# Selective scan: every fourth state's drive multiplied by POOL from a copy in SBUF

## The chip, the cores and the metric

The kernel runs on one core of a Trainium2 chip. The metric is the device time of one execution in microseconds; the median of several runs is compared. The engines are PE (TensorE), ACT (ScalarE), DVE (VectorE), POOL (GpSimd) and SP, which here only starts DMAs. They run their own instruction streams and meet at semaphores.

## What is computed

A hybrid layer: a gated selective scan, a feed-forward part with experts, a retention and attention part, and the feed-forward part again, each added to x. The change lies in the selective scan alone:

```python
def step(h, inp):
    dt_t, B_t, C_t, u_t = inp
    dA = jnp.exp(dt_t[..., None] * A)
    h = dA * h + (dt_t * u_t)[..., None] * B_t[:, None, :]
    y = jnp.einsum('bdn,bn->bd', h, C_t)
    return (h, y)
...
v = _silu(x_norm @ v1_w + v1_b)
return x_ssm * v @ w2_w + w2_b
```

There are 4 batches, 1024 time steps, 128 channels d and 16 states n. The second summand, (dt u) B, is called the drive below.

## The kernel before

The channels lie on the 128 partitions and time along the free dimension, so one batch's row is a tile of 128x1024 in f32. `selective_scan` handles one state of one batch after another, 64 in all. For each state n of a batch:

- PE spreads row n of B over the partitions into `drive_ps[n % 2]` (`spread_b`, L552; two PSUM tiles of 128x1024) and row n of C into `c_ps` (`spread_c`, L557). The selecting matrices and the rows are bf16.
- ACT makes `decay` = exp(dt a_n) in SBUF (L615) and copies `c_ps` into `c_rep` in SBUF (L619).
- DVE multiplies `drive_ps[n % 2]` by `du_t` = dt u in place, in PSUM (`drive`, L635), and then runs the scan over time (`scan`, L642) from `decay` (SBUF) and `drive_ps` (PSUM) into `state` (SBUF).
- POOL, which has access to SBUF alone here, multiplies `state` by `c_rep` into `hc` (L685).
- PE adds `hc` into `y_ps` by a product with the identity (`add_state`, three states later).

The order of each engine's work is written out by hand. DVE goes in pairs (`body`, L645): two scans, then the drives of the next two states. `spread_b` of state n waits until the scan of state n-2 has read the tile (L554), `spread_c` waits for ACT's copy of the state before. Count objects turn a batch and a state into the value that a semaphore must have. `pipelined` (L470) lets the last states of a batch overlap with the first ones of the next; at such a change of batch DVE also makes `y_sb` (L661), `yv` (L655) and the addition to x (L665), and PE the product with w2.

Beside it the expert weights are split into a high and a low f16 part, two experts a batch, at the states named in `SPLITS` = (3, 11): ACT's `enlarge` (L602) after its copy of c for state 3, ACT's `high_part` (L607) after that of state 4, POOL's `low_part` (L677) after `hc` of state 5, and the same from state 11. SP stores the result.

Semaphore waits stand in the stream of the waiting engine: what is behind a waiting instruction waits too.

Of the kernel before, what the change touches and what calls it, by code (L numbers as in the profile page):

```python
# [19 lines left out]
ALU = mybir.AluOpType  # L20
ACT = mybir.ActivationFunctionType
# [6 lines left out]
P = 128  # L28
B, T = 4, 1024
# [4 lines left out]
NS = 16  # L34
# [452 lines left out]
def selective_scan(t):  # L487
# [9 lines left out]
    with Stage(nc, "scan") as s:  # L497
        a_neg = s.sb("a_neg", [P, NS])
        dt_b = s.sb("dt_b", [P, T])
        decay = s.sb("decay", [P, 4, T])  # L500
        state = s.sb("state", [P, 2, T])
        c_rep = s.sb("c_rep", [P, 4, T])
        hc = s.sb("hc", [P, 4, T])
        y_sb = s.sb("y_sb", [P, T])
        yv = s.sb("yv", [P, T])
        w_raw, w_large = (s.sb(n, [P, 2, F]) for n in ("w_raw", "w_large"))
# [12 lines left out]
        dt_staged = s.count("dt_staged")  # L519
        decayed = s.count("decayed", NS, 1)  # L520
        c_copied = s.count("c_copied", NS, 1)
        driven = s.count("driven", NS)
        scanned = s.count("scanned", NS, 4)
        weighed = s.count("weighed", NS, 4)
        y_steps = s.count("y_steps", 2, 2)
        projected = s.count("projected", 1, 1)
        added = s.count("added", 1, 1)
        SPLITS = (3, 11)

        with nc.Block() as block:  # L530

# [57 lines left out]
            def _(act):  # L589
# [19 lines left out]
                with act.Fori(0, B) as b:  # L609
                    act.wait_ge(decayed.sem, decayed.before(b, 0, 1))  # L610
                    act.activation(dt_b[:, :], t.dt_t[:, b, :], ACT.Copy).then_inc(dt_staged.sem, 1)
                    act.wait_ge(dt_staged.sem, dt_staged.at(b))
                    for n in range(NS):
                        act.wait_ge(scanned.sem, scanned.before(b, n, 4))
                        act.activation(decay[:, n % 4, :], dt_b[:, :], ACT.Exp,  # L615
                                       scale=a_neg[:, n:n + 1]).then_inc(decayed.sem, 1)
                        act.wait_ge(c_spread.sem, c_spread.at(b, n))
                        act.wait_ge(weighed.sem, weighed.before(b, n, 4))
                        act.activation(c_rep[:, n % 4, :], c_ps[:, :], ACT.Copy).then_inc(c_copied.sem, 1)  # L619
                        if n in SPLITS:  # L620
                            enlarge(b, SPLITS.index(n))
                        if n - 1 in SPLITS:
                            high_part(b, SPLITS.index(n - 1), w_parts)
# [4 lines left out]
            def _(dve):  # L628
# [2 lines left out]
                dve.sem_inc(added.sem, added.start)  # L631

                def drive(b, n):
                    dve.wait_ge(b_spread.sem, b_spread.at(b, n))
                    dve.tensor_tensor(drive_ps[n % 2][:, :], drive_ps[n % 2][:, :], t.du_t[:, b + n // NS, :],  # L635
                                      ALU.mult).then_inc(driven.sem, 1)

                def scan(b, k):
                    dve.wait_ge(driven.sem, driven.at(b, k))
                    dve.wait_ge(decayed.sem, decayed.at(b, k))  # L640
                    dve.wait_ge(weighed.sem, weighed.before(b, k, 2))
                    dve.tensor_tensor_scan(state[:, k % 2, :], decay[:, k % 4, :], drive_ps[k % 2][:, :], 0.0,  # L642
                                           ALU.mult, ALU.add).then_inc(scanned.sem, 1)

                def body(b, n):  # L645
# [25 lines left out]
            def _(pool):  # L671
# [7 lines left out]

                with pool.Fori(0, B) as b:  # L680
                    for n in range(NS):
                        pool.wait_ge(scanned.sem, scanned.at(b, n))
                        pool.wait_ge(c_copied.sem, c_copied.at(b, n))
                        pool.wait_ge(summed.sem, summed.before(b, n, 4))
                        pool.tensor_tensor(hc[:, n % 4, :], state[:, n % 2, :], c_rep[:, n % 4, :],  # L685
                                           ALU.mult).then_inc(weighed.sem, 1)
                        if n - 2 in SPLITS:
                            low_part(b, SPLITS.index(n - 2), w_parts)
# [1266 lines left out]
```

## Time and profile before

| | us |
|---|---|
| median of 3 runs | 1385.3 (1382.85 to 1386.9) |
| the profiled execution | 1391.36 |
| its span | 1389.4 |
| scan stage in it, from the first drive to the last addition to x | 98.6 to 348.0 |
| DVE busy, 97.5 to 345.9 | 227.9 of 248.4 |
| POOL busy, the same stretch | 170.6 |
| ACT busy, the same stretch | 154.2 |
| PE busy, the same stretch | 195.0 |

The rows come from the page of the profile (groups of instructions, with the idle time of the engine just before them and what released it) and from answers of the trace (timelines: start, duration, engine, line, operation, output and inputs). Times are us from the span's start, means are ns. In a timeline an instruction marked x2 is two of them merged, with their common duration; two neighbours on one engine may overlap by some hundredths of a microsecond, so starts are subtracted rather than durations added.

### The profile page before, as it was taken

What the parts mean: (1) busy time and instruction counts of PE and PEld (TensorE: products, weight loads), DVE (VectorE), ACT (ScalarE), POOL (GpSimd) and SP (SyncE); (2) the same over time, 40 slices, a digit from 0 to 9 for tenths busy, and PEclk for the clock granted to TensorE, in tenths of its full rate; (3) what the DMA queues carried; (4) which work ended last, traced back from release to release, by engine and by line L of the source; (5) the groups of instructions that cost most, each with busy time, mean ns of one, the idle gap of its engine ahead of it and who ended that gap; (6) DMA issues with size and microseconds to landing.
All of it is one profiled execution on the core that took longest, in us unless ns stands there. A gap on an engine that the chain in (4) does not pass through costs nothing. (4 is left out here: it accounts for less than half of the span.)

```text
span 1389.4 us, 17492 instructions
## 1 busy us (share of the span) xinstructions
PE 1071.3 (77%) x5850; PEld 393.9 (28%) x5850; DVE 742.7 (53%) x1012; ACT 975.3 (70%) x884; POOL 325.7 (23%) x194
## 2 busy tenths in 40 slices
PE   4748777777799956777446888888888888679996
PEld 3213333333344422332341111111111111134443
DVE  5869998987566648998481001200300300256664
ACT  3767665754688832221336999999999999658885
POOL 3117776766111114665100000000000000011110
PEclk8769999999899978998777999999999999879998
DMA  2000100100100000000001111111111111000002
GB/s 73 0 16 30 31 30 30 60 30 31 32 30 30 31 24 0 0 0 1 8 0 33 24 24 32 37 24 28 22 33 34 24 24 28 11 31 31 30 30 61
DMA packets 24188, 36.48 MB, mean 26 GB/s; under 512 B 7362, under 2 KB 11970, under 8 KB 24130
## 3 DMA queue, kind: packets, MB, share of 16 engines
q1 hardware_dynamic: 24130, 35.71, 9.5%
q8 instruction: 36, 0.59, 0.2%
q14 instruction: 22, 0.18, 0.0%
HBM read 16.82 MB, written 6.29 MB: 17 GB/s over the span
## 5 line engine op out<-in xcount | busy, mean ns | idle before, releaser
L1674 ACT ACTIVATE att_prob<-att_s_ps 128x1536 f32<-128x1536 f32 x342 | 459.2, 1912 | 7.4 <-PE att_s_ps L1588 7.3
L1603 PE MATMUL att_o_ps<-att_prob,att_va 128*32 128x512 f32 x2048 | 273.9, 607 | 0.5 <-ACT att_prob L1674 0.5
L1705 DVE COPY att_o_sb<-att_o_ps 128x512 f32<-128x512 f32 x32 | 22.1, 691 | 381.7 <-PE att_o_ps L1603 381.7
L1588 PE MATMUL att_s_ps<-att_q_st,att_k_st 32*128 32x512 f16 x1024 | 134.4, 388 | 80.8 <-ACT att_prob L1674 76.1
L685 POOL TENSOR_TENSOR scan_hc<-scan_state,scan_c_rep 128x1024 f32<-128x1024 f32 x64 | 151.9, 2392 | 71.9 <-DVE scan_state L642 71.7
L787 POOL TENSOR_TENSOR ffn_veps<-ffn_mv,all_eps 128x4 f32<-128x4 f32 x16 | 9.1, 570 | 575.3 <-DVE ffn_mv L944 575.3
L642 DVE TENSOR_TENSOR_SCAN scan_state<-scan_decay,scan_drive_ps 128x1024 f32<-128x1024 f32 x64 | 142.9, 2270 | 0.3 <-ACT scan_decay L615 0.3
L282 PE MATMUL scan_y_ps<-scan_hc,all_ident 128*128 128x512 f32 x256 | 130.2, 634 | 8.3 <-DVE scan_y_sb L661 6.2
L1588 PEld LDWEIGHTS att_s_ps<-att_q_st,att_k_st 32*128 32x128 f16 x1024 | 33.1, 91 | 327.2 <-ACT att_prob L1674 315.9
L619 ACT ACTIVATE scan_c_rep<-scan_c_ps 128x1024 f32<-128x1024 f32 x64 | 65.4, 1022 | 80.4 <-PE scan_c_ps L282 80.1
L1012 DVE SCALAR_TENSOR_TENSOR ffn_hid_lo<-ffn_hid,ffn_share,ffn_hid_hi 128x1024 f16<-128x1024 f32 x64 | 81.9, 1283 | 48.8 <-ACT ffn_hid_hi L920 48.1
L1318 POOL TENSOR_TENSOR ret_qm<-ret_mem,ret_q_sb 128x1024 f32<-128x1024 f32 x32 | 74.5, 2350 | 67.0 <-DVE ret_mem L1270 64.0
L916 ACT ACTIVATE ffn_hid<-ffn_h_ps,ffn_be 128x1024 f32<-128x1024 f32 x64 | 71.1, 1111 | 21.7 <-PE ffn_h_ps L292 19.1
L635 DVE TENSOR_TENSOR scan_drive_ps<-scan_drive_ps,ssm_du_t 128x1024 f32<-128x1024 f32 x64 | 77.8, 1220 | 14.7 <-PE scan_drive_ps L282 14.4
L282 PE MATMUL scan_drive_ps<-ssm_bc,ssm_sel 96*128 (+1 forms) x128 | 41.4, 407 | 47.5 <-DVE scan_state L642 37.6
L292 PE MATMUL ffn_o_ps<-ffn_hid_hi,ffn_w_sel 128*128 128x512 f16 x256 | 76.0, 379 | 2.2 <-DVE ffn_hid_lo L1012 2.2
L920 ACT ACTIVATE ffn_hid_hi<-ffn_hid,ffn_share 128x1024 f16<-128x1024 f32 x64 | 73.5, 1149 | 4.9
L292 PE MATMUL ffn_h_ps<-ffn_z_hi,ffn_w_sel 128*128 (+1 forms) x256 | 76.2, 379 | 0.0
L615 ACT ACTIVATE scan_decay<-scan_dt_b,scan_a_neg 128x1024 f32<-128x1024 f32 x64 | 72.9, 1140 | 0.1
L1270 DVE TENSOR_TENSOR_SCAN ret_mem<-ret_g_sb,ret_kv_ps 128x1024 f32<-128x1024 f32 x32 | 71.2, 2266 | 0.0
L282 PEld LDWEIGHTS scan_y_ps<-scan_hc,all_ident 128*128 128x128 f32 x256 | 51.3, 202 | 55.5 <-issue 35.3
L1012 DVE SCALAR_TENSOR_TENSOR ffn_hid_lo<-ffn_hid,all_blend,ffn_hid_hi 128x1024 f16<-128x1024 f32 x32 | 42.9, 1341 | 44.4 <-ACT ffn_hid_hi L920 44.4
(215 smaller groups left out, 1505.8 us busy)
## 6 DMA issues: line engine op xcount, KB each, us to landing
ffn_w_sel<-w_split SPq DMA_DIRECT2D x16, 512.0 KB, 3.2
w_split<-scan_w_parts SPq DMA_DIRECT2D x8, 512.0 KB, 2.9
att_q_st<-hv_part SPq DMA_DIRECT2D x64, 64.0 KB, 2.1
att_k_st<-hv_part SPq DMA_DIRECT2D x64, 64.0 KB, 2.1
ln_x_half<-in_x SPq DMA_DIRECT2D x8, 256.0 KB, 2.8
scan_w_raw<-in_w1e SPq DMA_DIRECT2D x8, 256.0 KB, 3.2
scan_w_raw<-in_w2e SPq DMA_DIRECT2D x8, 256.0 KB, 3.4
out<-store_out SPq DMA_DIRECT2D x8, 256.0 KB, 2.4
```

The source lines that it names most:

```text
L282: last = pe.matmul(out[:, h], w, rhs[:, h], start=start, stop=stop)
L292: last = pe.matmul(out[:, h], w, x[:, h], start=start and i == 0, stop=stop and i == len(parts) - 1)
L615: act.activation(decay[:, n % 4, :], dt_b[:, :], ACT.Exp, scale=a_neg[:, n:n + 1]).then_inc(decayed.sem, 1)
L635: dve.tensor_tensor(drive_ps[n % 2][:, :], drive_ps[n % 2][:, :], t.du_t[:, b + n // NS, :], ALU.mult).then_inc(driven.sem, 1)
L642: dve.tensor_tensor_scan(state[:, k % 2, :], decay[:, k % 4, :], drive_ps[k % 2][:, :], 0.0, ALU.mult, ALU.add).then_inc(scanned.sem, 1)
L685: pool.tensor_tensor(hc[:, n % 4, :], state[:, n % 2, :], c_rep[:, n % 4, :], ALU.mult).then_inc(weighed.sem, 1)
L920: act.activation(hid_hi[:, m % 3, :], hid[:, m % 2, :], ACT.Copy, scale=weight_of_expert(k)).then_inc(casted.sem, 1)
L1012: dve.scalar_tensor_tensor(hid_lo[:, m % 3, :], hid[:, m % 2, :], weight_of_expert(m % M // FC), hid_hi[:, m % 3, :], ALU.mult, ALU.subtra ...
L1318: pool.tensor_tensor(qm[:, n, :], mem[:, n % 2, :], q_sb[:, :], ALU.mult).then_inc(weighed.sem, 1)
L1588: last = pe.matmul(s_ps[e % 2][:, n, :], k_st[rows, g % 2, kc * P:(kc + 1) * P], q_st[rows, g % 2, HALVES[half]], start=True, stop=True)
L1603: last = pe.matmul(o_ps[half][32 * j:32 * j + 32, :], va[:, g % 2, kc, j, :], prob[:, (GH * v + j) % RING, :], start=kc == 0, stop=kc == K ...
L1674: act.activation(prob[:, first % RING:first % RING + n, :], s_ps[e % 2][:, 0:n, :], ACT.Exp).then_inc(exped.sem, 1)
```

## The change

For the states 3, 7, 11 and 15 of each batch the drive no longer is DVE's. ACT copies the spread row from `drive_ps[1]` into a new SBUF tile `b_rep`, POOL multiplies it by `du_t` in place, and DVE's scan of that state reads `b_rep` instead of PSUM. The wait of `spread_b` on the scan two states before is as it was. There is one `b_rep`, so the four uses of a batch follow each other. `SPLITS` becomes (2, 10): enlarging after state 2, high part after 3, low part after 4.

```diff
+        b_rep = s.sb("b_rep", [P, T])
...
-        driven = s.count("driven", NS)
+        driven = s.count("driven", NS - NS // 4)
+        seen = s.sem("seen")
+        b_copied, pool_driven = s.count("b_copied", NS // 4), s.count("pool_driven", NS // 4)
...
-        SPLITS = (3, 11)
+        SPLITS = (2, 10)
+
+        def by_pool(n):
+            return n % 4 == 3
...
                         act.wait_ge(c_spread.sem, c_spread.at(b, n))
                         act.wait_ge(weighed.sem, weighed.before(b, n, 4))
+                        if by_pool(n):
+                            act.wait_ge(b_spread.sem, b_spread.at(b, n))
+                            act.activation(b_rep[:, :], drive_ps[n % 2][:, :], ACT.Copy).then_inc(b_copied.sem, 1)
                         act.activation(c_rep[:, n % 4, :], c_ps[:, :], ACT.Copy).then_inc(c_copied.sem, 1)
...
                 def drive(b, n):
+                    if by_pool(n):
+                        return
...
                 def scan(b, k):
-                    dve.wait_ge(driven.sem, driven.at(b, k))
+                    if by_pool(k):
+                        dve.wait_ge(pool_driven.sem, pool_driven.at(b, k // 4))
+                    else:
+                        dve.wait_ge(driven.sem, driven.at(b, k - k // 4))
                     dve.wait_ge(decayed.sem, decayed.at(b, k))
                     dve.wait_ge(weighed.sem, weighed.before(b, k, 2))
-                    dve.tensor_tensor_scan(state[:, k % 2, :], decay[:, k % 4, :], drive_ps[k % 2][:, :], 0.0,
+                    source = b_rep if by_pool(k) else drive_ps[k % 2]
+                    dve.tensor_tensor_scan(state[:, k % 2, :], decay[:, k % 4, :], source[:, :], 0.0,
...
                     for n in range(NS):
+                        if by_pool(n + 1):
+                            pool.wait_ge(b_copied.sem, b_copied.at(b, n // 4))
+                            pool.sem_inc(seen, 1)
+                            pool.tensor_tensor(b_rep[:, :], b_rep[:, :], t.du_t[:, b, :],
+                                               ALU.mult).then_inc(pool_driven.sem, 1)
                         pool.wait_ge(scanned.sem, scanned.at(b, n))
```

On DVE, in the middle of a batch, four states stand so before (names that end in 0 and 1 are the two PSUM tiles; an instruction named SCALAR_TENSOR_TENSOR with `scan_state` as output is the scan):

```order
L635 TENSOR_TENSOR scan_drive_ps0<-scan_drive_ps0,ssm_du_t 128x1024
L635 TENSOR_TENSOR scan_drive_ps1<-scan_drive_ps1,ssm_du_t 128x1024
L642 SCALAR_TENSOR_TENSOR scan_state<-scan_decay,scan_drive_ps0 128x1024
L642 SCALAR_TENSOR_TENSOR scan_state<-scan_decay,scan_drive_ps1 128x1024
L635 TENSOR_TENSOR scan_drive_ps0<-scan_drive_ps0,ssm_du_t 128x1024
L635 TENSOR_TENSOR scan_drive_ps1<-scan_drive_ps1,ssm_du_t 128x1024
L642 SCALAR_TENSOR_TENSOR scan_state<-scan_decay,scan_drive_ps0 128x1024
L642 SCALAR_TENSOR_TENSOR scan_state<-scan_decay,scan_drive_ps1 128x1024
```

and so with the change:

```order
L646 TENSOR_TENSOR scan_drive_ps0<-scan_drive_ps0,ssm_du_t 128x1024
L646 TENSOR_TENSOR scan_drive_ps1<-scan_drive_ps1,ssm_du_t 128x1024
L657 SCALAR_TENSOR_TENSOR scan_state<-scan_decay,scan_drive_ps0 128x1024
L657 SCALAR_TENSOR_TENSOR scan_state<-scan_decay,scan_drive_ps1 128x1024
L646 TENSOR_TENSOR scan_drive_ps0<-scan_drive_ps0,ssm_du_t 128x1024
L657 SCALAR_TENSOR_TENSOR scan_state<-scan_decay,scan_drive_ps0 128x1024
L657 SCALAR_TENSOR_TENSOR scan_state<-scan_decay,scan_b_rep 128x1024
```

The second drive of every other pair is gone, and the scan that it fed reads `b_rep`.

On POOL, states 10 to 15 of a batch stand so before:

```order
L685 TENSOR_TENSOR scan_hc<-scan_state,scan_c_rep 128x1024
L685 TENSOR_TENSOR scan_hc<-scan_state,scan_c_rep 128x1024
L685 TENSOR_TENSOR scan_hc<-scan_state,scan_c_rep 128x1024
L685 TENSOR_TENSOR scan_hc<-scan_state,scan_c_rep 128x1024
L677 TENSOR_TENSOR scan_w_parts<-scan_w_large,scan_w_parts 128x2x512
L685 TENSOR_TENSOR scan_hc<-scan_state,scan_c_rep 128x1024
L685 TENSOR_TENSOR scan_hc<-scan_state,scan_c_rep 128x1024
```

and so with the change:

```order
L700 TENSOR_TENSOR scan_b_rep<-scan_b_rep,ssm_du_t 128x1024
L705 TENSOR_TENSOR scan_hc<-scan_state,scan_c_rep 128x1024
L705 TENSOR_TENSOR scan_hc<-scan_state,scan_c_rep 128x1024
L705 TENSOR_TENSOR scan_hc<-scan_state,scan_c_rep 128x1024
L692 TENSOR_TENSOR scan_w_parts<-scan_w_large,scan_w_parts 128x2x512
L705 TENSOR_TENSOR scan_hc<-scan_state,scan_c_rep 128x1024
L700 TENSOR_TENSOR scan_b_rep<-scan_b_rep,ssm_du_t 128x1024
L705 TENSOR_TENSOR scan_hc<-scan_state,scan_c_rep 128x1024
L705 TENSOR_TENSOR scan_hc<-scan_state,scan_c_rep 128x1024
```

The product for state 11 stands ahead of `hc` of state 10, that for state 15 ahead of `hc` of state 14, and `low_part` moved from behind state 13 to behind state 12.

## Rows read from the trace of the kernel before

**Rows 1.** The page's groups: xcount | busy us, mean ns | idle before, releaser.
```profile
L685 POOL TENSOR_TENSOR scan_hc<-scan_state,scan_c_rep 128x1024 f32<-128x1024 f32 x64 | 151.9, 2392 | 71.9 <-DVE scan_state L642 71.7
...
L642 DVE TENSOR_TENSOR_SCAN scan_state<-scan_decay,scan_drive_ps 128x1024 f32<-128x1024 f32 x64 | 142.9, 2270 | 0.3 <-ACT scan_decay L615 0.3
...
L619 ACT ACTIVATE scan_c_rep<-scan_c_ps 128x1024 f32<-128x1024 f32 x64 | 65.4, 1022 | 80.4 <-PE scan_c_ps L282 80.1
...
L635 DVE TENSOR_TENSOR scan_drive_ps<-scan_drive_ps,ssm_du_t 128x1024 f32<-128x1024 f32 x64 | 77.8, 1220 | 14.7 <-PE scan_drive_ps L282 14.4
```

**Rows 2.** Timeline, 129 to 143 us: start, us, engine, instruction [idle before].
```profile
129.03 4.46 DVE L642 TENSOR_TENSOR_SCAN scan_state<-scan_decay,scan_drive_ps 128x1024 f32<-128x1024 f32 x2
...
133.40 2.42 DVE L635 TENSOR_TENSOR scan_drive_ps<-scan_drive_ps,ssm_du_t 128x1024 f32<-128x1024 f32 x2
...
133.95 0.60 PE L282 MATMUL scan_drive_ps<-ssm_bc,ssm_sel 96*128 x2
...
135.01 1.02 ACT L619 ACTIVATE scan_c_rep<-scan_c_ps 128x1024 f32<-128x1024 f32 x1 [0.52 <-PE scan_c_ps L282]
...
135.72 4.46 DVE L642 TENSOR_TENSOR_SCAN scan_state<-scan_decay,scan_drive_ps 128x1024 f32<-128x1024 f32 x2
...
138.08 4.69 POOL L685 TENSOR_TENSOR scan_hc<-scan_state,scan_c_rep 128x1024 f32<-128x1024 f32 x2 [2.02 <-DVE scan_state L642]
...
140.05 1.05 ACT L607 ACTIVATE scan_w_parts<-scan_w_large 128x1024 f16<-128x1024 f32 x1
...
142.04 1.01 ACT L619 ACTIVATE scan_c_rep<-scan_c_ps 128x1024 f32<-128x1024 f32 x1
...
142.43 4.45 DVE L642 TENSOR_TENSOR_SCAN scan_state<-scan_decay,scan_drive_ps 128x1024 f32<-128x1024 f32 x2
```

**Rows 3.** Timeline at two changes of batch, DVE and PE.
```profile
173.43 4.45 DVE L642 TENSOR_TENSOR_SCAN scan_state<-scan_decay,scan_drive_ps 128x1024 f32<-128x1024 f32 x2
...
177.52 2.68 PE L282 MATMUL scan_y_ps<-scan_hc,all_ident 128*128 128x512 f32 x4
...
231.90 1.23 DVE L635 TENSOR_TENSOR scan_drive_ps<-scan_drive_ps,ssm_du_t 128x1024 f32<-128x1024 f32 x1 [1.87 <-PE scan_drive_ps L282]
...
234.24 4.46 DVE L642 TENSOR_TENSOR_SCAN scan_state<-scan_decay,scan_drive_ps 128x1024 f32<-128x1024 f32 x2
```

**Rows 4.** Timeline of POOL, `low_part` behind a pair of `hc`.
```profile
149.42 2.13 POOL L677 TENSOR_TENSOR scan_w_parts<-scan_w_large,scan_w_parts 128x1024 f16<-128x1024 f32 x1
```

**Rows 5.** Instructions of line 413: duration in ns, minimum/median/maximum, first and last start.
```profile
L413 DVE TENSOR_SCALAR conv_y<-conv_x,all_vec x4: 753/1380/2370, 37.0 to 68.6; 128x1024 f32<-128x1024 f32 x4
```

**Rows 6.** Timelines of DVE and POOL around 68, 166, 373 and 402 us.
```profile
68.09 2.34 POOL L467 TENSOR_TENSOR ssm_du_t<-ssm_dt_t,ssm_u_t  x1 [11.41 <-DVE ssm_dt_t L446]
68.61 2.37 DVE L413 TENSOR_SCALAR conv_y<-conv_x,all_vec 128x1024 f32<-128x1024 f32 x1 [0.82 <-ACT conv_x L376]
...
166.01 1.20 DVE L655 TENSOR_TENSOR scan_yv<-scan_y_sb,ssm_v_t 128x1024 f32<-128x1024 f32 x1
...
166.31 3.11 POOL L685 TENSOR_TENSOR scan_hc<-scan_state,scan_c_rep 128x1024 f32<-128x1024 f32 x1 [3.20 <-DVE scan_state L642]
...
372.24 1.25 DVE L1012 SCALAR_TENSOR_TENSOR ffn_hid_lo<-ffn_hid,all_blend,ffn_hid_hi 128x1024 f16<-128x1024 f32 x1
372.40 1.15 POOL L787 TENSOR_TENSOR ffn_veps<-ffn_mv,all_eps 128x4 f32<-128x4 f32 x1 [18.57 <-DVE ffn_mv L944]
373.62 1.01 POOL L789 TENSOR_TENSOR ffn_rstd<-ffn_veps,all_minus_half 128x4 f32<-128x4 f32 x1
374.76 0.41 DVE L952 TENSOR_SCALAR ffn_z_tok<-ffn_tok_ps,ffn_mv,ffn_rstd 128x128 f32<-128x128 f32 x1 [1.27 <-POOL ffn_rstd L789]
...
401.73 1.28 DVE L1012 SCALAR_TENSOR_TENSOR ffn_hid_lo<-ffn_hid,all_blend,ffn_hid_hi 128x1024 f16<-128x1024 f32 x1
...
402.10 3.12 POOL L798 TENSOR_TENSOR all_x_t<-all_x_t,ffn_y 128x1024 f32 x1 [20.98 <-DVE ffn_y L1006]
...
404.74 1.57 DVE L1012 SCALAR_TENSOR_TENSOR ffn_hid_lo<-ffn_hid,all_blend,ffn_hid_hi 128x1024 f16<-128x1024 f32 x1 [1.60 <-ACT ffn_hid_hi L920]
```

**Rows 7.** Busy us by stretch: length, PE, PEld, DVE, ACT, POOL, then the granted clock.
```profile
172.00:176.00 4.00, 1.53 (x5) 0.25 (x4) 4.00 (x4) 1.79 (x2) 0.22 (x1) 0.96 0.00 0
176.00:180.00 4.00, 4.00 (x8) 1.68 (x8) 3.00 (x2) 2.33 (x3) 4.00 (x2) 0.61 0.00 0
```

## Prediction

> **What bounds the kernel now.** The scan stage is read alone: it runs from about 98 to 348 us of a span of 1389.4 us, and every later stage waits for it. The grouped lines of the page [rows 1] show the stage's large items: 64 scans of 2270 ns and 64 drives of 1220 ns on DVE, 64 products `hc` of 2392 ns on POOL. The idle column tells who bounds it. The scans waited 0.3 us in total, so nothing keeps them; the drives waited 14.4 us for TensorE, while POOL waited 71.7 us for DVE's scans. The timeline of two pairs [rows 2] shows the beat: two scans from 129.03, two drives from 133.40, two scans from 135.72, two from 142.43. That is 6.70 us for two states, 13.40 for four, with DVE never idle. A drive is worth 1.16 us of it (2.32 from 133.40 to 135.72), a scan 2.19. POOL has 2.0 us of slack in each pair. So a drive taken from DVE is worth at most 1.16 us x 16 = 18.6 us. The question is whether its result arrives in time by the other road.
>
> At each change of batch there is more: the scan pairs that start at 173.43 and 234.24 [rows 3] are 60.81 apart. Three plain groups of four take 40.2 of it, which leaves 20.6 for the group that holds y_sb, yv and x_t (some 3.5 us of work, each at the pace of a drive) and waits of drives for TensorE, the larger 1.87 us.
>
> **The new road, step by step.** Call the four states 0 to 3, and count from the end of scan 1. In each group bmul 3 (the product on POOL) must come before scan 3.
>
> First, TensorE may write `drive_ps1` for state 3 only when scan 1 has read it; that wait is unchanged. In [rows 2] scan 1 ends at 133.49, the spread of b ends at 134.55, that of c somewhat later, and ACT's copy begins at 135.01: 1.52 after. When ACT has an extra weight step first, the copy begins at 142.04 against a scan end of 140.19: 1.85 after. The new copy of b takes that place and costs 1.02 (the copy of c, same form). Add 0.1 for a semaphore: bmul 3 can start at 2.65, or 2.97 with the weight step.
>
> Second, POOL must be free. hc 0 and hc 1 start 2.1 before the end of scan 1 and last 4.69 [rows 2], so POOL is free at 2.6: a tie with ACT. In every other group, though, `low_part` (2.13, [rows 4]) now stands between hc 0 and hc 1 and ends up ahead of bmul: 2.6 + 2.13 = 4.7. It was harmless in the 2 us of slack.
>
> Third, bmul 3 has the form of du_t on POOL, 2.34 us [rows 6]. Without anything else scan 3 would start 0.12 later (POOL to DVE, from 373.62 + 1.01 to 374.76 in [rows 6]). DVE by then has only drive 2 and scan 2 to do, until about 3.5, against 5.1 or 7.2 for bmul's end. **DVE waits in every group**, where before it waited in none. The cover that would be needed isn't there.
>
> Fourth, the scan's sources. Scan 3 now reads decay and `b_rep`, both in SBUF, and POOL's next instruction, hc 2, is ready as soon as bmul ends. No scan with two SBUF inputs stands in this trace, so I take the nearest rows. yv on DVE (two SBUF inputs) started at 166.01 and ran its 1.20; hc started at 166.31 and took 3.11, about 0.77 more than its usual. The product L798 started 0.37 behind another such DVE instruction and took 3.12 instead of 2.34. The other way round, the DVE instruction at 404.74 found L798 running until 405.22 and took 1.57 instead of 1.28; it ended 1.09 after POOL. All this is in [rows 6]. The plainest is 68.61: a DVE instruction that takes 0.75 at the least [rows 5] lasted 2.37, until POOL's du_t (68.09 to 70.43) was over. While one runs the other stands still, and the first one wins. Scans that read PSUM run beside hc in every pair of [rows 2] with no loss on either side.
>
> The Trainium skill says the same in "SBUF — State Buffer", section "Who interferes with whom": a DVE instruction with two SBUF inputs contends with a GpSimd instruction that reads SBUF, by an exclusive lock, and issue order decides who blocks. This case's rows agree (0.77 us lost by hc beside yv), for tensor_tensor; no run here shows it for a scan. By that rule scan 3 or hc 2 waits; without it the time would be that of the third case below.
>
> Fifth, who comes first. hc follows hc with no gap (two in 4.69 [rows 2]), a DVE instruction starts 0.12 behind the POOL result that it waits for. In [rows 6] a head start of 0.16 us (372.24 against 372.40) was enough to win. So I take it that hc 2 starts ahead of scan 3 and scan 3 stands for the whole of it.
>
> **The sum of one group.** bmul and hc 2 are 2 x 2.34 = 4.68; the scan ends 2.27 less the 0.19 of start that overlaps (1.28 - 1.09) = 2.08 later; two drives and two scans follow as now, 6.70. Together 13.46. With the lead of 2.97 (bmul 3 and 11 of a batch, which have the enlarging ahead of them) this is 16.4, with 4.7 (bmul 7 and 15) 18.15. Against 13.40 that is +3.0 and +4.75.
> - 8 groups with low_part: 8 x 4.75 = 38.0
> - bmul 11 in 4 batches and bmul 3 in the first: 5 x 3.0 = 15.0
> - the 3 groups over a batch change: y_sb and most of yv now lie in DVE's new idle time. Their road is 16.4 + x_t 1.2 + a clash of yv with bmul or hc, 1.1 = 18.7 if TensorE makes no stall, 20.6 if its first one stays; I take 19.7 against 20.6, so 3 x -0.9 = -2.7
> - TensorE's clock: granted 0.96 over 172 to 176, while PE was busy 1.53 of 4 us, and 0.61 over the next 4 us [rows 7], so mostly at the lower level (1.2 GHz); the additions of one state took 2.68 there [rows 3]. Now PE is idle some 4 to 5 us in every group, so such falls will come in most groups. Low_part's delay covers a later copy in half of them. I take +3, with bounds 0 and 15 (2 us, about the stall of 1.87 in [rows 3], in the 7 or 8 groups not covered).
>
> Sum: 38.0 + 15.0 - 2.7 + 3 = **+53 us**. The 16 more ACT copies (16 us) lie in ACT's idle time (80.1 us waiting for c_ps [rows 1]) but for the 1.02 already on the road; moving the weight steps one state earlier is in the leads; the ACT copy of c for state 3 comes 1.0 later and is wanted only by hc 3, 5 us on. Nothing outside the stage changes, so later stages move by that amount. The profiled execution took 1391.4 and would take 1444; the median is 6.1 lower, 1385.3 + 53 = **1438 us**. With the clock term at its bounds and the batch changes at theirs, 1432 to 1453.
>
> **Rivals.**
> - Scan 3 gets ahead of hc 2. Then it starts 0.12 after bmul, and hc 2 stands for 2.2 us instead. The group is 2.34 + 0.12 + 2.19 + 6.70 = 11.35 plus the lead: 14.3 or 16.05, +0.9 and +2.65. POOL's own load is then five products, the standstill and every other time low_part, 13.9 or 16.05, so it is as late as the road: +18 to +33, taken as +27, **1412 us**. Against it: POOL's start is 0.12 ahead.
> - No contention for a scan at all, since a scan takes 2.27 us for what a product does in 1.22 and its second input might come otherwise. Same leads: 8 x 2.65 + 5 x 0.9 = 25.7, and the batch changes gain 2.5 each by hidden y_sb and yv: +18, **1403 us**. Against it are the rows of yv and of 404.74.
> - The change does what it says, faster: DVE stays the bound and loses 16 drives, -18.6, **1367 us**. It needs bmul's end before 3.5 after scan 1, so the copy, or the spread of b, would have to be done 1.5 us sooner than the rows allow; it would decide if POOL's product or its queue were that much shorter. Nothing in the profile speaks for it save that DVE is saturated.
> - No change: hidden stalls at the batch changes outweigh +0.9 and +2.65 in the third case; would need +18 to vanish, **1385 us**.
>
> **How the numbers follow.** Forecast 0.70 (1432 to 1453, most of it), scan first 0.12, no contention 0.11, faster 0.04, same 0.03. Range: the forecast's upper bound 1453, with 3 us for the runs' own spread (1382.85 to 1386.9), so 1456, and down to 1402, which takes in the scan-first case and about half of the third; some 0.85 together, less what the sizes may miss. About 0.3% (4 us) is what a measurement of this kernel can tell from no change: faster 0.04, same 0.03, slower 0.93.
>
> **What would show it.** In the profile after: scans with `b_rep` some 4.4 us long in the forecast (2.27 in the third case, with hc 2 at 4.5 in the second); POOL's bmul directly followed by hc 2; DVE idle before these scans, released by POOL, some 2.0 us in half of the groups and 3.7 in the others (leads of 2.97 and 4.7, plus 2.34 and 0.12, less the 3.5 that drive 2 and scan 2 fill), about 40 us in all; pairs of groups 16.4 and 18.2 apart; PE clock below 0.93 in the stage. The forecast is wrong if the b_rep scans last 2.3 us, or if DVE doesn't wait for POOL before them.

## The result, and the profile after

The changed kernel takes 1437.8 us (median of 4 runs, 1435.39 to 1441.01) against 1386.1 us for the kernel before on the same chip: a ratio of 1.038, with an interval of 1.0364 to 1.0397. The change costs 51.7 us. The profiled execution of the changed kernel took 1438.1 us with a span of 1436.1 us. That of the kernel before, at 1391.4 us, was some 5 us above its median, so the two spans differ by 46.7 us only.

First the groups of the profile page that answer to [rows 1]. The columns are count, busy us and mean ns, then idle time before them and what ended it; the last line is from the list of waits (in total, times, longest).

```profile
L705 POOL TENSOR_TENSOR scan_hc<-scan_state,scan_c_rep 128x1024 f32<-128x1024 f32 x64 | 153.3, 2401 | 79.2 <-DVE scan_state L657 76.9
L628 ACT ACTIVATE scan_c_rep<-scan_c_ps 128x1024 f32<-128x1024 f32 x64 | 65.4, 1022 | 106.7 <-PE scan_c_ps L282 106.5
L657 DVE TENSOR_TENSOR_SCAN scan_state<-scan_decay,scan_drive_ps 128x1024 f32<-128x1024 f32 x48 | 107.8, 2272 | 1.5 <-ACT scan_decay L621 0.3
L657 DVE TENSOR_TENSOR_SCAN scan_state<-scan_decay,scan_b_rep 128x1024 f32<-128x1024 f32 x16 | 70.0, 4375 | 40.3 <-POOL scan_b_rep L700 40.3
```

```profile
DVE scan_state L657 <- POOL scan_b_rep L700: 40.3, 13, 3.6
```

The 48 scans that read PSUM take 2272 ns, as the 64 did before. The 16 that read `b_rep` take 4375 ns: 2.1 us more each, 33.7 in all. Ahead of 13 of them DVE stands idle, 40.3 us in all, released by POOL's product. Before, the scans waited 0.3 us in total. The longer scans and the waits ahead of them add 74 us together. Three `yv`, one at each change of batch, now stand beside POOL's product and add another 3. Against that, 18.6 us of drives are gone from DVE, and the drives' waits for TensorE fell from 14.4 to 4.8 us. The sum is 48.8 us; the stage, from the first drive to the last addition to x, grew by 49.7, from 249.4 us to 299.1.

The timeline shows both in two groups of four states, in time order by engine (start us, duration us, engine, instruction; the last bracket is idle time before). The group of states 4 to 7 begins at 118.04, that of 8 to 11 at 136.07, that of 12 to 15 at 152.83. They answer to [rows 2] and [rows 4].

```profile
118.04 4.45 DVE L657 TENSOR_TENSOR_SCAN scan_state<-scan_decay,scan_drive_ps 128x1024 f32<-128x1024 f32 x2
120.39 2.35 POOL L705 TENSOR_TENSOR scan_hc<-scan_state,scan_c_rep 128x1024 f32<-128x1024 f32 x1 [2.08 <-DVE scan_state L657]
122.69 2.13 POOL L692 TENSOR_TENSOR scan_w_parts<-scan_w_large,scan_w_parts 128x1024 f16<-128x1024 f32 x1
124.78 2.36 POOL L705 TENSOR_TENSOR scan_hc<-scan_state,scan_c_rep 128x1024 f32<-128x1024 f32 x1
125.80 1.02 ACT L627 ACTIVATE scan_b_rep<-scan_drive_ps 128x1024 f32<-128x1024 f32 x1 [2.22 <-PE scan_c_ps L282]
127.08 2.37 POOL L700 TENSOR_TENSOR scan_b_rep<-scan_b_rep,ssm_du_t 128x1024 f32<-128x1024 f32 x1
129.40 2.36 POOL L705 TENSOR_TENSOR scan_hc<-scan_state,scan_c_rep 128x1024 f32<-128x1024 f32 x1
129.57 4.33 DVE L657 TENSOR_TENSOR_SCAN scan_state<-scan_decay,scan_b_rep 128x1024 f32<-128x1024 f32 x1 [3.56 <-POOL scan_b_rep L700]
...
136.07 4.45 DVE L657 TENSOR_TENSOR_SCAN scan_state<-scan_decay,scan_drive_ps 128x1024 f32<-128x1024 f32 x2
138.40 0.77 PE L282 MATMUL scan_drive_ps<-ssm_bc,ssm_sel 96*128 x2 [0.46 <-DVE scan_state L657]
142.55 1.01 ACT L627 ACTIVATE scan_b_rep<-scan_drive_ps 128x1024 f32<-128x1024 f32 x1
143.75 2.35 POOL L700 TENSOR_TENSOR scan_b_rep<-scan_b_rep,ssm_du_t 128x1024 f32<-128x1024 f32 x1 [0.64 <-ACT scan_b_rep L627]
146.22 4.34 DVE L657 TENSOR_TENSOR_SCAN scan_state<-scan_decay,scan_b_rep 128x1024 f32<-128x1024 f32 x1 [2.16 <-POOL scan_b_rep L700]
152.83 4.46 DVE L657 TENSOR_TENSOR_SCAN scan_state<-scan_decay,scan_drive_ps 128x1024 f32<-128x1024 f32 x2
...
178.65 2.35 POOL L700 TENSOR_TENSOR scan_b_rep<-scan_b_rep,ssm_du_t 128x1024 f32<-128x1024 f32 x1 [0.46 <-ACT scan_b_rep L627]
179.86 2.23 DVE L670 TENSOR_TENSOR scan_yv<-scan_y_sb,ssm_v_t 128x1024 f32<-128x1024 f32 x1
180.97 3.33 POOL L705 TENSOR_TENSOR scan_hc<-scan_state,scan_c_rep 128x1024 f32<-128x1024 f32 x1
182.01 4.44 DVE L657 TENSOR_TENSOR_SCAN scan_state<-scan_decay,scan_b_rep 128x1024 f32<-128x1024 f32 x1
```

POOL goes from bmul to the next `hc` without a gap and starts it at 129.40. The scan, released by the same bmul, starts at 129.57, 0.17 later, and is done at 133.90; `hc` was done at 131.76 and took its normal time. So DVE stood for 2.1 us while POOL lost nothing. Of the 16 scans from `b_rep`, 9 start 0.16 to 0.17 us behind an `hc`, 4 start 0.07 to 0.08 behind it, and the three at the changes of batch 1.04 to 1.05; all 16 take 4.33 to 4.44. In the first group `low_part` (122.69) has put bmul off, and bmul follows an `hc` at once; in the second, POOL had 0.64 us to wait for ACT's copy. The last four lines are the change of batch: yv took 2.23 us instead of 1.20 beside bmul, and `hc` behind it 3.33.

The granted clock of TensorE over the same groups, by stretches of 4 us (busy us of PE, PEld, DVE, ACT, POOL, then the clock), answers to [rows 7]:

```profile
144.00:148.00 4.00, 2.76 (x8) 1.00 (x8) 1.84 (x2) 4.00 (x5) 4.00 (x2) 1.00 0.00 0
148.00:152.00 4.00, 1.39 (x4) 0.56 (x5) 4.00 (x3) 0.41 (x1) 1.77 (x2) 0.63 0.00 0
152.00:156.00 4.00, 4.00 (x8) 1.46 (x7) 4.00 (x3) 2.06 (x2) 1.80 (x2) 0.52 0.01 2
156.00:160.00 4.00, 4.00 (x14) 1.90 (x13) 3.88 (x3) 2.63 (x3) 4.00 (x3) 1.00 0.00 0
```

PE stands idle during the long scan, since the spread that is next in its queue waits for the end of that scan. The clock falls to its lower level (1.2 GHz), and by 156 us it is back at the higher (2.4 GHz). This recurs in nearly every group; over the stage the granted clock averages 0.86, against 0.93 before.

### The profile page after: what moved, and what is told of

Same layout as the page of the kernel before. It is cut to its first block and busy times, and to the rows that moved or that the text cites. A ratio compares the mean times of both kernels' runs of the same rounds, so it can differ in the third digit from the quotient of the medians.

```text
span 1436.1 us, 17589 instructions
## 1 busy us (share of the span) xinstructions
PE 1087.5 (76%) x5850; PEld 394.9 (27%) x5850; DVE 762.8 (53%) x996; ACT 988.5 (69%) x900; POOL 363.7 (25%) x210
## 5 line engine op out<-in xcount | busy, mean ns | idle before, releaser
L705 POOL TENSOR_TENSOR scan_hc<-scan_state,scan_c_rep 128x1024 f32<-128x1024 f32 x64 | 153.3, 2401 | 79.2 <-DVE scan_state L657 76.9
L282 PE MATMUL scan_y_ps<-scan_hc,all_ident 128*128 128x512 f32 x256 | 142.8, 687 | 9.3 <-POOL scan_hc L705 6.7
L657 DVE TENSOR_TENSOR_SCAN scan_state<-scan_decay,scan_drive_ps 128x1024 f32<-128x1024 f32 x48 | 107.8, 2272 | 1.5 <-ACT scan_decay L621 0.3
L282 PE MATMUL scan_drive_ps<-ssm_bc,ssm_sel 96*128 (+1 forms) x128 | 44.9, 436 | 78.0 <-DVE scan_state L657 67.5
L657 DVE TENSOR_TENSOR_SCAN scan_state<-scan_decay,scan_b_rep 128x1024 f32<-128x1024 f32 x16 | 70.0, 4375 | 40.3 <-POOL scan_b_rep L700 40.3
L936 ACT ACTIVATE ffn_hid<-ffn_h_ps,ffn_be 128x1024 f32<-128x1024 f32 x64 | 71.2, 1112 | 21.7 <-PE ffn_h_ps L292 18.8
L282 PEld LDWEIGHTS scan_y_ps<-scan_hc,all_ident 128*128 128x128 f32 x256 | 54.4, 216 | 63.3 <-issue 40.6
L818 POOL TENSOR_TENSOR all_x_t<-all_x_t,ffn_y 128x1024 f32 (+1 forms) x8 | 23.4, 2930 | 177.4 <-DVE ffn_y L1026 177.4
```

Of the source, the lines that this page charges most:

```text
L282: last = pe.matmul(out[:, h], w, rhs[:, h], start=start, stop=stop)
L936: act.activation(hid[:, m % 2, :], h_ps[m % 2][:, :], ACT.Gelu_apprx_tanh, bias=b1, scale=1.0 / WS).then_inc(gelued.sem, 1)
```

## The experiments

The theory has three parts: the road to bmul's end (the spread, ACT's copy, POOL's queue) is longer than the work DVE has; a scan with two SBUF inputs stands still beside an `hc` that began first; and the falling clock is a small addition. The rivals: a scan from SBUF is slow by itself; the moved weight steps cost the time; or the multiplication alone is what comes too late. In the recorded expectations f1 to f7 are the runs 1 to 7 below, g1 is run 8, h1 run 9 and g2 run 10; "the port" in them is what DVE and POOL contend for.

**1. `hc` ahead of bmul.** POOL's two instructions change places, so that nothing of POOL's runs beside the scan of `b_rep`.

```diff
-                        if by_pool(n + 1):
-                            pool.wait_ge(b_copied.sem, b_copied.at(b, n // 4))
-                            ... (bmul)
                         pool.wait_ge(scanned.sem, scanned.at(b, n))
...
+                        if by_pool(n + 1):
+                            pool.wait_ge(b_copied.sem, b_copied.at(b, n // 4))
+                            ... (bmul)
```

> POOL does hc of state 2 ahead of the product for state 3, so nothing on POOL is ready when scan 3 starts. Theory (POOL's hc 2 holds up a scan with two SBUF inputs): the 16 scans from b_rep take 2.27 us instead of 4.33, but start later, 8.4 us (9.5 with low_part) after the end of scan 1; groups of four 17.3 and 18.4 us, the time about 1447. Rival (a scan with two SBUF inputs is slow by itself): they still take 4.3 us, groups 19.4 and 20.5, about 1480.

Measured: 1447.4 us (1445.07 to 1450.05), ratio 1.045 (1.0422 to 1.0481). The grouped lines of this kernel over the stage (L705 is bmul in it), and its timeline:

```profile
L657 DVE TENSOR_TENSOR_SCAN scan_state<-scan_decay,scan_b_rep 128x1024 f32<-128x1024 f32 x16 | 36.7, 2292 | 85.1 <-POOL scan_b_rep L705 85.1
```

```profile
133.60 4.45 DVE L657 TENSOR_TENSOR_SCAN scan_state<-scan_decay,scan_drive_ps 128x1024 f32<-128x1024 f32 x2
143.97 2.34 POOL L705 TENSOR_TENSOR scan_b_rep<-scan_b_rep,ssm_du_t 128x1024 f32<-128x1024 f32 x1
146.44 2.29 DVE L657 TENSOR_TENSOR_SCAN scan_state<-scan_decay,scan_b_rep 128x1024 f32<-128x1024 f32 x1 [4.86 <-POOL scan_b_rep L705]
150.89 2.28 DVE L657 TENSOR_TENSOR_SCAN scan_state<-scan_decay,scan_drive_ps 128x1024 f32<-128x1024 f32 x1
```

POOL is idle during all 16 of these scans, and the same scan takes 2.29 us. A scan from SBUF is not slow by itself; the 4.33 are `hc` beside it. What is gained there is lost in front: the wait grows to 85.1 us, and the group from 133.60 to 150.89 is 17.29 long where it was 16.76.

**2. `hc` held back.** POOL's `hc` of state 2 waits until scan 3 is done, and bmul keeps its place.

```diff
-                        pool.wait_ge(scanned.sem, scanned.at(b, n))
+                        pool.wait_ge(scanned.sem, scanned.at(b, n + 1 if by_pool(n + 1) else n))
```

> POOL's hc of state 2 (6, 10, 14) waits until scan 3 (7, 11, 15) is done, with the product where the change has it. Theory: the b_rep scans take 2.27 us and DVE's wait for POOL stays at about 40 us; groups 14.3 and 16.1 us against 16.8 and 18.1, the time 30 us less than the changed kernel, about 1408. Rival (the wait for the product is the whole cost, and the long scan costs nothing since hc would be late otherwise): hc 2 pushed back makes the next scans late, time within 8 us of 1438.

Measured: 1422.9 us (1421.56 to 1427.91), ratio 1.0265 (1.0241 to 1.0290): 15 us back, half of what was expected. The scans take 2288 ns again. The rest is in the timeline:

```profile
130.54 9.55 POOL L705 TENSOR_TENSOR scan_hc<-scan_state,scan_c_rep 128x1024 f32<-128x1024 f32 x4 [2.49 <-DVE scan_state L657]
132.95 3.78 PE L282 MATMUL scan_y_ps<-scan_hc,all_ident 128*128 128x512 f32 x4 [0.54 <-POOL scan_hc L705]
136.52 0.92 PE L282 MATMUL scan_drive_ps<-ssm_bc,ssm_sel 96*128 x2
140.82 1.01 ACT L627 ACTIVATE scan_b_rep<-scan_drive_ps 128x1024 f32<-128x1024 f32 x1
142.01 2.36 POOL L700 TENSOR_TENSOR scan_b_rep<-scan_b_rep,ssm_du_t 128x1024 f32<-128x1024 f32 x1 [1.91 <-ACT scan_b_rep L627]
```

The late `hc` 2 is added to y by PE at 132.95, at the lower clock (3.78 us for four matmuls that take 1.88 at the higher), and the spread of the next pair's b stands behind it in PE's queue until 136.52. ACT's copy and the next bmul are late by that; POOL waits 1.91 for the copy. The wait for bmul grew from 40.3 to 45.5 us. The larger part of the missing 15 us is another wait for late additions: `y_sb`, which needs the last of them, waits 14.3 us for TensorE instead of 5.0. I had not counted that the held instruction has a consumer ahead of the road.

**3. The weight steps alone.** The kernel before with `SPLITS = (2, 10)` and nothing else.

```diff
-        SPLITS = (3, 11)
+        SPLITS = (2, 10)
```

> The kernel before with SPLITS (2, 10) alone. Theory: the move of the weight steps by itself is cheap, 0 to 4 us more than 1386 (only the wait for a later copy of c, half a microsecond in 7 groups); DVE's waits before drives and scans stay under 20 us. Rival (the move is a large part of the loss): 10 us or more.

Measured: 1384.4 us (10 runs), ratio 0.9993 (0.9982 to 1.0004). The moved steps cost nothing by themselves. That they cost something where bmul comes behind them is what run 4 tests.

**4. `low_part` out of the road.** The changed kernel with `SPLITS = (1, 9)`, so that `low_part` stands one state earlier, behind an `hc` after which POOL has slack.

```diff
-        SPLITS = (2, 10)
+        SPLITS = (1, 9)
```

> The change with SPLITS (1, 9): low_part now stands behind hc of state 3 (11), where POOL waits for scan 4 anyway, and no longer between hc 4 and the product for state 7. Theory: groups with 18.1 us fall to 16.1 to 16.8, 1.3 to 2.0 us in 8 groups, the time 11 to 16 us under the changed kernel, about 1424. Rival (ACT's copy or TensorE at its lower clock is as late as POOL in those groups): under 5 us.

Measured: 1430.0 us (1429.09 to 1431.82), ratio 1.032 (1.0295 to 1.0345): 8 us back instead of 11 to 16. Where `low_part` had been, groups fell from 18.1 to 16.2 (151.43 to 167.60), as expected. But two of the three groups behind a change of batch take 19.1 and 19.2 us (the third takes 16.3). This is one of them:

```profile
190.44 3.62 PE L282 MATMUL scan_y_ps<-scan_hc,all_ident 128*128 128x512 f32 x4
193.86 1.01 PE L282 MATMUL scan_drive_ps<-ssm_bc,ssm_sel 96*128 x2
196.54 2.36 POOL L700 TENSOR_TENSOR scan_b_rep<-scan_b_rep,ssm_du_t 128x1024 f32<-128x1024 f32 x1 [3.17 <-ACT scan_b_rep L627]
199.02 4.33 DVE L657 TENSOR_TENSOR_SCAN scan_state<-scan_decay,scan_b_rep 128x1024 f32<-128x1024 f32 x1 [4.69 <-POOL scan_b_rep L700]
```

There the clock is at 0.50 (188 to 192 us), the additions take 3.62 us, and the spread of b comes behind them. In the changed kernel the additions are as slow at this place (3.21 us, from 187.31), but the wait for bmul is 3.57 us as in every other group with `low_part`: POOL was as late anyway. So `low_part` had covered most of this cost of the clock.

**5. No product at all.** bmul is left out and the scan reads ACT's copy of the spread row, so the states that depend on it are other numbers; the time is that of the road with a free multiplication.

```diff
-                        dve.wait_ge(pool_driven.sem, pool_driven.at(b, k // 4))
+                        dve.wait_ge(b_copied.sem, b_copied.at(b, k // 4))
...
-                        if by_pool(n + 1):
-                            ... (bmul)
```

> POOL's product with du_t is left out: the scan of every fourth state reads ACT's copy of the spread row as it is. Theory (the road by POOL is too long by its 2.34 us, and whoever starts first wins): the copy is done 2.6 to 3.0 us after the end of scan 1, before DVE is through with scan 2, so scan 3 starts behind scan 2, 0.1 to 0.2 us ahead of hc 2, takes 2.27 us, and hc 2 takes 4.4. DVE waits only where TensorE is at its lower clock; the time 1376 to 1385. Rival (POOL's hc gets the port whatever the order, or POOL becomes the bound): the scans take over 4 us, time about 1400.

Measured: 1394.7 us (1393.14 to 1398.31), ratio 1.0072 (1.0051 to 1.0094), where 1376 to 1385 was expected. A miss: even with the product for nothing the kernel is slower than before. Four of the 16 scans take 2.27 us, twelve 4.3 to 4.45 (mean 3879 ns). One of each kind:

```profile
121.27 4.67 POOL L700 TENSOR_TENSOR scan_hc<-scan_state,scan_c_rep 128x1024 f32<-128x1024 f32 x2
123.66 4.43 DVE L657 TENSOR_TENSOR_SCAN scan_state<-scan_decay,scan_b_rep 128x1024 f32<-128x1024 f32 x1 [1.16 <-POOL scan_hc L700]
...
138.15 2.27 DVE L657 TENSOR_TENSOR_SCAN scan_state<-scan_decay,scan_b_rep 128x1024 f32<-128x1024 f32 x1
138.32 9.05 POOL L700 TENSOR_TENSOR scan_hc<-scan_state,scan_c_rep 128x1024 f32<-128x1024 f32 x3 [1.04 <-DVE scan_state L657]
```

At 138.15 the scan is 0.17 us ahead: it runs its 2.27, and POOL's three `hc` take 9.05 instead of 7.0. At 123.66 it waits for `hc` 1, since it overwrites the state that `hc` 1 reads; POOL's `hc` 2 follows `hc` 1 at once (it ends at 125.94 and takes 2.35, so it began at 123.59), 0.07 us ahead of the scan, and the scan stands for the whole of it. So there is a second way to lose the race, without bmul: 8 of the 12 long scans waited for a late `hc` 1 like this one. The four that win are those of state 11, one in each batch. The groups show what the race is worth: those of states 8 to 11, where the scan wins, take 12.4 us against 13.40 before, about the drive that was saved; those of states 4 to 7 and 12 to 15, where it loses, take 15.7.

**6. `low_part` early, and PE's spread first.** As 4, and TensorE writes the spreads of states 3, 7, 11 and 15 before the addition of the state before.

```diff
-                    if n >= LAG and there(b, n - LAG, NS):
-                        add_state(b, n - LAG)
+                    for m in ((n - 1, n) if by_pool(n) else () if by_pool(n + 1) else (n,)):
+                        if m >= LAG and there(b, m - LAG, NS):
+                            add_state(b, m - LAG)
```

> The change with SPLITS (1, 9), as in f4, and PE spreads b and c of states 3, 7, 11, 15 ahead of the addition of the state before, not behind it. Theory (in f4 the copy of b in some groups is late because the spread stands behind a y addition of 3.6 us at TensorE's lower clock; DVE waited up to 4.7 us there): the wait falls to about 2 us in all groups, groups 16.1 to 16.5 us, the time 5 to 8 us under f4, about 1424. Rival (the y additions become late and POOL waits for them): no gain over 1430.

Measured: 1427.0 us (1424.62 to 1433.77), ratio 1.030 (1.0272 to 1.0332), not distinct from run 4; 5 to 8 us less was expected. The groups are 16.6, also behind a change of batch, and the waits for bmul fell to 27.8 us. But the additions are late at the change itself:

```profile
DVE scan_y_sb L677 <- PE scan_y_ps L282: 13.3, 4, 4.5
```

```profile
176.91 1.28 DVE L677 SCALAR_TENSOR_TENSOR scan_y_sb<-ssm_u_t,all_vec,scan_y_ps 128x1024 f32<-128x1024 f32 x1 [3.50 <-PE scan_y_ps L282]
```

The first line is from the list of waits, the second from the timeline. y_sb waits 3.5 us for PE there, and the group from 167.83 to 189.23 is 21.4 long where run 4 has 18.75. What the order gave, it took back.

**7. Both remedies.** Run 2's hold and run 6's order of PE, with `SPLITS = (2, 10)`.

> f2 (hc 2 held until scan 3 is done) with the same order on PE as f6. Theory (what f2 gained by scans of 2.29 us it lost since hc 2 came later, and PE's addition of it stood ahead of the next spreads): the copy of b no longer waits for it; groups with no low_part fall from 16.3 to about 14.5, the others to 16.1; the time 1410 to 1415 against 1423. Rival (DVE's own wait for hc 2 before scan 4, and POOL's four products in a row, set it): 1420 or more.

Measured: 1420.4 us (1418.81 to 1424.32), ratio 1.0254 (1.0231 to 1.0277), where 1410 to 1415 was expected; 2.5 us under run 2. The waits for bmul are still 41.5 us, and `y_sb` waits 16.7. With scans of 2.29 us the road still takes longer than DVE's work. These runs didn't find an order that makes it short enough while TensorE's tile for state 3 is free only at the end of scan 1.

**8. A road that doesn't wait for the tile, for states 7 and 15.** The row of b for state 7 (15) is spread into `c_ps` behind state 0 (8), ACT copies it to one of two `b_rep` tiles, POOL multiplies it in an earlier slot; the tile `drive_ps` is not used by these states. `SPLITS` is (1, 9). The lines shown are against the changed kernel.

```diff
-            return n % 4 == 3
+            return n % 8 == 7
...
+                    if more and n % 8 == 0:
+                        pe.wait_ge(c_copied.sem, c_copied.at(b, n))
+                        product(pe, c_ps, t.sel[:, n % NS + 7, :], t.bc[:, b + n // NS, :]).then_inc(early_spread.sem, 1)
...
+                        if n % 8 == 0:
+                            act.wait_ge(early_spread.sem, early_spread.at(b, n // 8))
+                            act.activation(b_rep[:, n // 8, :], c_ps[:, :], ACT.Copy).then_inc(b_copied.sem, 1)
...
-                        if by_pool(n + 1):
-                            pool.wait_ge(b_copied.sem, b_copied.at(b, n // 4))
+                        if n % 8 == 2:
+                            pool.wait_ge(b_copied.sem, b_copied.at(b, n // 8))
```

> The drive of every eighth state only (7 and 15), with its row of b spread into c_ps behind state 0 (8), so that ACT copies and POOL multiplies it five states ahead; two tiles b_rep; SPLITS (1, 9). Theory (the idea fails only by its road and by who comes first at the port): DVE never waits for the product, the b_rep scan starts behind scan 6, 0.18 us ahead of hc 6, and takes 2.27; 8 drives of 1.16 us go, 1377, up to 5 us more by the extra copies in the c chain. Rival (POOL has no slack left for 3.1 more products' worth of time, or the standstill of hc 6 makes DVE wait): 1386 or more.

Measured: 1384.4 us (12 runs, 1378.66 to 1388.85), ratio 0.9979 (0.9962 to 0.9997), where 1377, up to 5 us more, was expected. The grouped line and the timeline:

```profile
L665 DVE TENSOR_TENSOR_SCAN scan_state<-scan_decay,scan_b_rep 128x1024 f32<-128x1024 f32 x8 | 18.1, 2266 | 0.0
```

```profile
104.22 1.23 DVE L654 TENSOR_TENSOR scan_drive_ps<-scan_drive_ps,ssm_du_t 128x1024 f32<-128x1024 f32 x1 [4.80 <-PE scan_drive_ps L282]
...
126.70 2.27 DVE L665 TENSOR_TENSOR_SCAN scan_state<-scan_decay,scan_b_rep 128x1024 f32<-128x1024 f32 x1
126.86 6.57 POOL L713 TENSOR_TENSOR scan_hc<-scan_state,scan_c_rep 128x1024 f32<-128x1024 f32 x2 [0.63 <-DVE scan_state L665]
130.50 1.23 DVE L654 TENSOR_TENSOR scan_drive_ps<-scan_drive_ps,ssm_du_t 128x1024 f32<-128x1024 f32 x1 [0.41 <-PE scan_drive_ps L282]
```

This is the change as it was meant: DVE doesn't wait for the product, the scan is 0.16 us ahead of `hc`, and POOL takes the standstill in its slack (6.57 for two `hc`, 1.9 more than usual). Eight drives of 1.16 us should give 9.3. The stage is 3.6 us shorter in the profile (245.8 against 249.4): one drive at the stage's head waits 4.80 us, where before it waited 0.47, since its spread stands behind the early one in PE's queue, and behind seven of these eight scans a drive waits 0.4 to 1.2 for its spread. In all the drives wait 17.7 us for TensorE instead of 14.4, and the last y_sb 7.6 instead of 5.7. By the medians 0.7 us is left, and the interval ends just short of no change.

**9. The same road for all states of the change.** As 8, for states 3, 7, 11 and 15; the early spread stands behind states 0, 4, 8 and 12.

```diff
-            return n % 8 == 7
+            return n % 4 == 3
...
-                        if n % 8 == 2:
+                        if n % 4 == 1:
```

> g1's early road for all of the change's states (3, 7, 11, 15): the b row is spread into c_ps behind state 0 of the group, copied by ACT and multiplied by POOL three states ahead; SPLITS (1, 9). Theory (the change has three costs: a result that comes too late, a port held at the wrong time, and more work than POOL has room for): the first is gone, scans from b_rep start in time; but POOL then has five products of 2.34 and, where the scan starts first, a standstill of 2.2 in each four states, 13.9 us (16.0 in every second group, with low_part), more than the 13.40 of before; POOL is the bound and the time is 1395 to 1410. Rival (only lateness counts): DVE is the bound, 16 drives go, 1370 to 1378.

Measured: 1419.4 us (1419.25 to 1420.11), ratio 1.0236 (1.0217 to 1.0254), where 1395 to 1410 was expected. The scans take 4403 ns and DVE waits 18.9 us for POOL, but not for the product:

```profile
126.39 2.35 POOL L710 TENSOR_TENSOR scan_b_rep<-scan_b_rep,ssm_du_t 128x1024 f32<-128x1024 f32 x1
128.70 4.67 POOL L715 TENSOR_TENSOR scan_hc<-scan_state,scan_c_rep 128x1024 f32<-128x1024 f32 x2
131.09 4.42 DVE L667 TENSOR_TENSOR_SCAN scan_state<-scan_decay,scan_b_rep 128x1024 f32<-128x1024 f32 x1 [1.38 <-POOL scan_hc L715]
```

bmul is done at 128.7, ahead of the 129.7 at which DVE is ready. Now `hc` 1 is late behind it, the scan waits for `hc` 1, `hc` 2 follows `hc` 1 at 131.02, and the scan loses the race by 0.07 us, as in run 5. All 16 scans are long here too. In the rows of run 8 POOL has idled 0.63 us ahead of the `hc` beside the scan and is woken by a scan; in those of run 9 it goes from `hc` 0 through bmul, `hc` 1 and `hc` 2 without a pause. Two things differ between the runs, how often bmul comes and where it stands, and they aren't separated. The next group shows that POOL still has idle time elsewhere:

```profile
133.79 1.02 ACT L638 ACTIVATE scan_b_rep<-scan_c_ps 128x1024 f32<-128x1024 f32 x1 [1.13 <-PE scan_c_ps L282]
135.60 2.36 POOL L715 TENSOR_TENSOR scan_hc<-scan_state,scan_c_rep 128x1024 f32<-128x1024 f32 x1 [2.23 <-DVE scan_state L667]
140.04 2.35 POOL L715 TENSOR_TENSOR scan_hc<-scan_state,scan_c_rep 128x1024 f32<-128x1024 f32 x1 [2.08 <-DVE scan_state L667]
```

ACT's copy is done at 134.81, and POOL then idles 2.08 us ahead of `hc` 0. By these rows a bmul (2.35 us) placed there would make `hc` 1 some 0.3 us late, in the groups without `low_part`; that is an estimate. No run has it, so it isn't shown that the early road must fail for all four states.

**10. Run 8 with its spread of states 1 and 9 freed.** PE's wait of these spreads is put four scans back instead of two.

```diff
-                    pe.wait_ge(scanned.sem, scanned.before(b, n, 2))
+                    pe.wait_ge(scanned.sem, scanned.before(b, n, 4 if n % 8 == 1 else 2))
```

> g1 with the spread of b for states 1 and 9 waiting for the scan four states before instead of two, since the tile that it fills was not used by state 7 (15). Theory (g1's missing gain is in DVE's waits for this spread, 0.4 to 1.2 us behind each b_rep scan): they go, 3 to 5 us less than g1, 1379 to 1381. Rival (TensorE's lower clock at the batch changes or POOL sets the time): no change against g1, 1384.

Measured: 1386.9 us (12 runs), ratio 1.0006 (0.9993 to 1.0018), where 1379 to 1381 was expected. The drives wait as they did, 17.4 us in all. PE's rows tell why:

```profile
128.97 0.60 PE L282 MATMUL scan_c_ps<-ssm_bc,ssm_sel 96*128 x2
129.41 0.59 PE L282 MATMUL scan_drive_ps<-ssm_bc,ssm_sel 96*128 x2
```

The spread at 129.41 follows the early spread (128.97) directly, and that one waits for ACT to read `c_ps` (the copy of c began at 127.45 and takes 1.02). It is the queue that holds it, not its own semaphore. Of all versions only run 8 has an interval below 1, by 0.03% at its upper end, and run 10, which should have been faster still, is at 1.0006: no gain is shown.

## Why the prediction was right, point by point

The time (1437.8 against a forecast of 1438), its sign and the mechanism hold. By the steps:

- **First and second, when bmul starts.** With `low_part`, 4.7 us after scan 1: measured 4.6 (122.49 to 127.08). Without it 2.97: measured 3.2 (140.52 to 143.75). Of the 0.26, 0.16 is the pair's first spread, for which PE took 0.77 us (the row at 138.40) instead of 0.61 and behind which ACT's row of instructions up to the copy begins; most of the rest is a semaphore of 0.19 (143.56 to 143.75) where 0.1 was taken.
- **Third, DVE waits in every group.** 3.7 and 2.0 us were forecast, some 40 in all. Measured 3.56, 2.16, and 40.3. At the three changes of batch it doesn't wait, as the forecast had y_sb and yv lie there.
- **Fourth and fifth, the scan stands for the whole of `hc` 2.** 4.4 us forecast, 4.33 to 4.44 measured; `hc` is 0.17 ahead in the groups shown, where 0.12 was taken. Run 1 shows the reason: the same scan at 2.29 us with POOL idle. In run 5 the scan wins with 0.17 in hand and loses by 0.07. One of the rows behind this step was read too widely: the instruction at 68.61, called the plainest case, has one tile as input and so isn't of the form in question; the rows of yv and of 404.74 are. The two rivals of this step are out by it: the changed kernel has the long scan 16 times of 16, and the case without contention has scans of 2.27.
- **The rule cited.** The Trainium skill, "SBUF — State Buffer", section "Who interferes with whom", says that a DVE instruction with two SBUF inputs contends with a GpSimd instruction that reads SBUF, and that issue order decides which of them blocks. The trace agrees, for a scan too: 4.33 us behind an `hc` that began first, and 2.29 in run 1 with POOL idle.
- **The sum.** From the starts of the groups' first scans, in us:

| Groups | Forecast, more than before | Measured |
|---|---|---|
| states 0 to 3 of the first batch | 3.0 | 3.8 |
| states 4 to 7 of the first batch | 4.75 | 4.5 |
| states 8 to 11, four times | 12.0 | 13.3 (16.5 to 16.8 against 13.40) |
| states 12 to 15, three times | 14.25 | 13.9 (18.06 to 18.15 against 13.5) |
| states 12 to 15 of the last batch, to the stage's end | 4.75 | 3.9 |
| change of batch with states 4 to 7 behind it, three times | 11.55 | 10.4 |
| clock | 3 | in the rows above |
| sum | 53 | 49.7 (249.4 to 299.1) |

So the mechanism is right and several terms were mis-sized: too much for the clock (3), the changes of batch (1.1) and the end of the last batch (0.9), too little for the groups of states 8 to 11 (1.3) and the first group (0.8). They cancel in part and leave the stage 3.6 us under the sum, which was 53.3 before rounding. That the median comes within 0.2 us of 1438 is luck. The clock's 3 us of their own weren't needed: the granted clock fell in nearly every group, to 0.86 over the stage, but what it delayed was mostly the additions, behind the spreads; it shows in the 0.3 us by which the groups of states 8 to 11 exceed 16.4, perhaps in part of the 0.8 of the first group (not separated). Run 4 shows what it can cost where nothing covers it, about 3 us in each of two groups. And at the changes of batch the forecast put both stalls of drives (0.56 and 1.67 us before, of which the second lies in the group behind) into one group of 20.6; measured, the changing group went from 17.5 to 18.9 us at the first change and from 18.8 to 18.8 at the others, and the one behind from 15.1 to 18.1. Forecast together with the group behind, +3.85 each; measured +4.5, +2.8 and +3.2.

The medians differ by 51.7, the stage by 49.7 in the two profiled executions. The one of the kernel before was 5.3 us above its median; outside the stage it took 3.0 us more than that of the changed kernel. The remaining 2 us may lie in its stage. They are within what single executions of either kernel differ by, and stay unexplained.

## What to carry to other kernels

Before an instruction is taken from a saturated engine, compare when its result can be there by the new road with when that engine wants it: here the tile was free at the end of scan 1, DVE wanted the product 3.5 us later, and spread, copy, POOL's queue and product took 5.6 to 7 us. Moving its input to SBUF makes the consumer a rival of POOL; whether it pays then hangs on who starts first. Each time that a scan from `b_rep` was woken by POOL and POOL had its next instruction ready, POOL's started first: 13 of 13 in the changed kernel and 13 of 13 in run 9. A product made five states earlier, for two states of a batch and where POOL still idles, costs nothing and here gains nothing that is shown.

## What the runs showed of the hardware that was not expected

- How little decides who stands: 0.16 to 0.17 us ahead, a scan kept its 2.27 us (runs 5 and 8); 0.07 us behind, it took 4.4 (runs 5 and 9). In none of the rows shown do both sides lose a part of one encounter.
- The winner may be either side in the same kernel: in run 5, the four scans of state 11 won and the twelve others lost, eight of them behind a late `hc` 1 in the groups with `low_part`.
- The loser's price is nearly the same on either side, 2.0 to 2.2 us for a scan (4.33 to 4.44 against 2.27 to 2.29) and 1.9 for an `hc` (6.57 for two in run 8), but POOL's is hidden in its slack (no wait of DVE in run 8), and DVE's is not.
